# First attention: queries and keys as two fp32r parts, scores on alternating halves of the array's rows

## The reference, cut to what matters

```python
qkv = (x @ Wqkv.T + bqkv).reshape(Bb, Ss, 3, H, HD).transpose(2, 0, 3, 1, 4)
q, k, v = (qkv[0], qkv[1], qkv[2])
attn = jax.nn.softmax(jnp.einsum('bhid,bhjd->bhij', q, k) / jnp.sqrt(jnp.float32(HD)), axis=-1)
...
mod = attn * coh[..., None]
mod = mod / (mod.sum(-1, keepdims=True) + 1e-08)
...
mod = (1.0 - fi) * mod + fi * fa[:, None, :, None]
out = jnp.einsum('bhij,bhjd->bhid', mod, v).transpose(0, 2, 1, 3).reshape(Bb, Ss, Ee)
return out @ Wout.T + bout
```

## Time and profile before

| what | value |
|---|---|
| median of 3 runs | 1663.36 us (1662.22 to 1663.41) |
| the profiled execution's own time | 1665.16 us |
| its span (first to last instruction) | 1663.2 us |
| TensorE busy, share of the span | 1511.5 us, 91% |
| VectorE, ScalarE, POOL busy | 1050.4, 903.7, 496.5 us |
| granted TensorE clock over the span | 0.966 |
| projection | 0 to 105 us |
| first attention | 105.5 to 475.1 us |

### The profile page before, as it was taken

How to read it: one execution, slowest core, us unless ns; L and a number is a source line. 1 busy time by engine, 2 the same in 40 slices (tenths; PEclk the granted TensorE clock), 3 DMA queues, 4 the chain that set the end, 5 groups by cost and what they waited for, 6 DMA issues and landing times. The chain is left out here.

```text
span 1663.2 us, 24878 instructions
## 1 busy us (share of the span) xinstructions
PE 1511.5 (91%) x9076; PEld 988.6 (59%) x9076; DVE 1050.4 (63%) x1915; ACT 903.7 (54%) x1870; POOL 496.5 (30%) x299
## 2 busy tenths in 40 slices
PE   7889999999977999999997689997799689997898
PEld 3432222222234888887874467776577477776676
DVE  3768888888637556464555355555777455555786
ACT  5147777777742434343432487876433477776342
POOL 7100000000015100000002487775312487775113
PEclk9899999999989999999998899999799799999899
DMA  8721212200000330303005200001100100000010
GB/s 244 138 39 20 35 26 39 39 1 1 1 24 2 127 102 5 109 0 114 0 0 174 70 1 1 1 1 49 28 1 0 58 1 2 1 1 26 1 50 25
DMA packets 59312, 64.84 MB, mean 39 GB/s; under 512 B 15091, under 2 KB 48579, under 8 KB 59221
## 3 DMA queue, kind: packets, MB, share of 16 engines
q1 hardware_dynamic: 57860, 60.24, 14.3%
q10 hardware_dynamic: 1360, 3.41, 0.6%
HBM read 52.95 MB, written 10.49 MB: 38 GB/s over the span
## 5 line engine op out<-in xcount | busy, mean ns | idle before, releaser
L577 DVE TENSOR_REDUCE mcol<-bank 128x1 f32<-128x1024 f32 x256 | 302.1, 1217 | 58.5 <-PE bank L568 58.4
L662 ACT ACTIVATE a_pt<-bank 128x512 f32<-128x512 f32 x512 | 266.4, 603 | 89.0 <-PE bank L694 88.9
L694 PE MATMUL bank<-qa,ka 99*128 99x512 bf16 x512 | 193.8, 386 | 7.6 <-ACT a_pt L662 3.8
L568 PE MATMUL bank<-ka,qa 96*128 96x512 bf16 x512 | 193.7, 386 | 5.6 <-DMA ka<-k_parts 2.1
L1639 DVE CUSTOM_DVE_ANT_0 w_sm<-bank,mask 128x256 f32<-128x256 f32 (+1 forms) x256 | 89.0, 404 | 147.5 <-PE bank L1473 147.5
L1831 PE MATMUL bank<-m_hn,m_w 128*128 128x512 f32 x576 | 150.9, 419 | 19.0 <-DVE m_hn L1962 16.4
L1436 PE MATMUL bank<-wqkv,w_hst 128*128 128x512 f32 x576 | 156.4, 420 | 12.5 <-DVE w_sinp L1616 7.6
L694 PEld LDWEIGHTS bank<-qa,ka 99*128 99x128 bf16 x512 | 49.2, 98 | 165.7 <-ACT a_pt L662 121.3
L1831 PEld LDWEIGHTS bank<-m_hn,m_w 128*128 128x128 f32 x576 | 112.4, 196 | 56.0 <-issue 27.2
L705 PE MATMUL bank<-a_pt,vst 128*32 128x512 f32 x1024 | 136.4, 605 | 0.1
L1564 ACT ACTIVATE w_sm<-w_sm,w_st 128x256 f32<-128x256 f32 (+1 forms) x256 | 124.0, 489 | 19.2 <-DVE w_st L1639 19.0
(11 more groups left out here) (231 smaller groups left out, 2766.6 us busy)
## 6 DMA issues: line engine op xcount, KB each, us to landing
f_wex<-in_W SPq DMA_DIRECT2D x8, 2048.0 KB, 12.0
qa<-q_parts SPq DMA_DIRECT2D x48, 128.0 KB, 4.5
ka<-k_parts SPq DMA_DIRECT2D x48, 128.0 KB, 4.7
q_parts<-p_parts SPq DMA_DIRECT2D x16, 192.0 KB, 3.3
k_parts<-p_parts SPq DMA_DIRECT2D x8, 384.0 KB, 3.4
wqkv_raw<-in_wqkv SPq DMA_DIRECT2D x2, 1536.0 KB, 8.8
w<-in_w SPq DMA_DIRECT2D x2, 1536.0 KB, 6.4
phi<-in_phi SPq DMA_DIRECT2D x5, 512.0 KB, 3.6
```

What stands on the lines that cost most here:

```text
L568: last = nc.tensor.matmul(max_bank(G, r)[:, jh * HALF:(jh + 1) * HALF], G["qa"][k][0:KS, hg % 2, h, it * P:(it + 1) * P], G["ka"][k][0:KS, ...
L577: nc.vector.reduce_max(G["mcol"][hg % 2][:, p:p + 1], max_bank(G, r)[:, :], X).then_inc(G["max_free"], 1)
L662: nc.scalar.activation(pt[n % 2][:, q, :], sbank(HG * step + q), ACT.Exp, scale=HD0 ** -0.5).then_inc(p_ready, 1)
L694: mm(sbank(i), ka[k][:, q, n * P:(n + 1) * P], qa[k][:, ih, q, :], start=True, stop=True).then_inc(st_ps, 1)
```

## The change

Queries and keys are written in two fp32r parts, high and rest, in place of three of bf16, and three products of parts in place of six: 3 x 16 = 48 partitions, with two rows of maxima 50. These 50 fit in half of the array's rows. So `qa` holds all queries twice, on partitions 0 to 49 and 64 to 113, and `ka` holds the first 512 keys of a group on the lower half and the last 512 on the upper. The matmuls of a maxima pair go to one half each. The scores of the attention come from the lower and the upper half in turn, the upper lagging two behind; the order of the key tiles in the weighted sum changes with it, and `a_pt` has three buffers. What each engine does is re-ordered accordingly.

ScalarE's second part and POOL's third go; the split of the maxima has two operations for four, and four row DMAs for three. Loads of a group are again twelve DMAs, of fp32; those of the first group go in units 4 to 9. The ones of the keys' side are written over 32 partitions on each half; those of the fourth group (now a buffer that is allocated after the projection) at the start of the attention, and TensorE and SP wait for them there. `p_c1T` lies over the ring of parts, so ScalarE waits for the stores before it writes there.

```diff
-KS = 6 * HD0
-KA = KS + 3
-Q_PART = (0, 0, 1, 1, 0, 2)
-K_PART = (0, 1, 0, 1, 2, 0)
+KS = 3 * HD0
+KA = KS + 2
+ROWS = P // 2
+Q_PART = (0, 0, 1)
+K_PART = (0, 1, 0)
...
-        parts = sb("p_parts", [P, 4, 3, HALF], BF16)
+        parts = sb("p_parts", [P, 4, 2, HALF], F32R)
...
+                sp.wait_ge(G["ones_in"], 2 * GB)
                 for u, (b, hf, m) in enumerate(UNITS):
-                    sp.wait_ge(qk_p3, u + 1)
+                    sp.wait_ge(qk_low, u + 1)
...
-                    if u >= 4:
+                    if 4 <= u < 4 + 2 * len(Q_PART):
                         load_head_parts(sp, G, u % 2, 0, 0, ((u - 4) // 2,))
...
-                for u in range(len(UNITS)):
-                    pool.wait_ge(qk_p2, u + 1)
-                    nc.gpsimd.tensor_tensor(parts[:, u % 4, 2, :], rest[:, u % 4, :], parts[:, u % 4, 1, :],
-                                            ALU.subtract).then_inc(qk_p3, 1)
+                for s in range(GB - 1):
+                    write_ones(nc, pool, G, s)
...
+                for s in range(4):
+                    act.wait_ge(qk_stored[s], STORED[s] * len(UNITS) // 4)
...
+def write_ones(nc, pool, G, k):
+    for d in range(2):
+        nc.gpsimd.memset(G["ka"][k][ROWS * d + 32:ROWS * d + 64, :, :].bitcast(F32), 1.0).then_inc(G["ones_in"], 1)
...
-        last = nc.tensor.matmul(max_bank(G, r)[:, jh * HALF:(jh + 1) * HALF], G["qa"][k][0:KS, hg % 2, h, it * P:(it + 1) * P],
-                                G["ka"][k][0:KS, h, jh * HALF:(jh + 1) * HALF], start=True, stop=True)
+        rows = slice(ROWS * jh, ROWS * jh + KS)
+        last = nc.tensor.matmul(max_bank(G, r)[:, jh * HALF:(jh + 1) * HALF], G["qa"][k][rows, hg % 2, h, it * P:(it + 1) * P],
+                                G["ka"][k][rows, h, :], start=True, stop=True)
...
-        pt = [sb(f"a_pt{s}", [P, HG, HALF]) for s in range(2)]
+        pt = [sb(f"a_pt{s}", [P, HG, HALF]) for s in range(3)]
...
+        EACH = PAIRS * HALVES
+        LAG = 2
...
+        def units(e):
+
+            return [(d, x) for d, x in ((0, e), (1, e - LAG)) if 0 <= x < EACH]
...
+                write_ones(nc, pool, G, GB - 1)
+                pool.wait_ge(G["ones_in"], 2 * GB + 2)
...
+                for e in range(EACH + LAG):
+                    for d, x in units(e):
+                        i, tile = turn_of(d, x), tile_of(d, x)
+                        if tile >= 3 and x % HG == 0:
+                            act.wait_ge(pv_done, tile - 2)
+                        act.wait_ge(st_ps, i + 1)
+                        nc.scalar.activation(pt[tile % 3][:, x % HG, :], sbank(i), ACT.Exp,
+                                             scale=HD0 ** -0.5).then_inc(p_ready, 1)
...
                     if i >= 3:
                         pe.wait_ge(p_ready, i - 2)
-                    mm(sbank(i), ka[k][:, q, n * P:(n + 1) * P], qa[k][:, ih, q, :],
+                    rows = slice(ROWS * d, ROWS * d + KA)
+                    mm(sbank(i), ka[k][rows, q, n * P:(n + 1) * P], qa[k][rows, ih, q, :],
                        start=True, stop=True).then_inc(st_ps, 1)
...
-                pe.wait_ge(G["ones_in"], GB + 2)
...
+                pe.wait_ge(G["ones_in"], 2 * GB + 2)
+                for e in range(EACH + LAG + HG + 1):
+                    hg, x = e // PAIRS, e % PAIRS
+                    ahead, p = (hg + 1, x + EARLY) if x + EARLY < PAIRS else (hg + 2, x + EARLY - PAIRS)
+                    for d, y in units(e):
+                        scores(d, y)
+                    if x == EARLY + 2 and hg + 1 < HALVES:
+                        maxima_to_rows(nc, pe, G, hg + 1)
+                    if ahead < HALVES:
+                        score_pair(nc, pe, G, ahead, p)
+                    if e % 2 == 1 and e >= HG + 1 and (e - HG - 1) // 2 < TT * HALVES:
+                        weighted((e - HG - 1) // 2)
```

More of the change, by code:

```diff
@@ L117, in stage_project @@
         sgn = sb("p_sgn", [16, 16])
[L119 to L121 removed]
+        with nc.sbuf_tensor("p_c1T", [P, KD, N], F32) as c1T:
+            pass
+        parts = sb("p_parts", [P, 4, 2, HALF], F32R)
         cbias = sb("p_cbias", [P, KD, B])
@@ L273, in _ @@
                         nc.scalar.activation(qsd[:, :, :], qn[:, :, :], ACT.Sqrt).then_inc(q_sd, 1)
-                second(len(UNITS) - 1)
                 act.wait_ge(ln_var, 1)
@@ L631, in stage_attention0, with turn_of, tile_of, filled @@
         obank = PB[1][:, HALF:T]
+        EACH = PAIRS * HALVES
+        LAG = 2
+        def turn_of(d, e):
+            return e + max(0, e - LAG) if d == 0 else min(e + LAG + 1, EACH) + e
+        def tile_of(d, e):
+            return e // HG * 2 + d
+        def filled(tile):
+            return turn_of(tile % 2, tile // 2 * HG + HG - 1) + 1
+        def units(e):
+            return [(d, x) for d, x in ((0, e), (1, e - LAG)) if 0 <= x < EACH]
         with nc.Block() as block:
@@ L702, in weighted @@
                             pe.wait_ge(o_out, hg)
-                    pe.wait_ge(p_ready, HG * (step + 1))
+                    pe.wait_ge(p_ready, filled(tile))
                     for q in range(HG):
-                        last = mm(obank[32 * q:32 * q + 32, :], vst[hg // 2 % 2][:, jt, q, :],
-                                  pt[jt % 2][:, q, :], start=(jt == 0), stop=(jt == TT - 1))
+                        last = mm(obank[32 * q:32 * q + 32, :], vst[hg // 2 % 2][:, jt % 2 * (TT // 2) + jt // 2, q, :],
+                                  pt[tile % 3][:, q, :], start=(jt == 0), stop=(jt == TT - 1))
                     last.then_inc(pv_done, 1)
-                pe.wait_ge(G["ones_in"], GB + 2)
-                for hg in range(HALVES):
-                    pe.wait_ge(G["shifted"][hg // 2 % GB], 48 * (2 * (hg // (2 * GB)) + hg % 2 + 1))
-                    for n in range(TT):
-                        ahead = hg + 1 if n < TT // 2 else hg + 2
-                        p0 = (2 * n + EARLY) % PAIRS
-                        for q in range(HG):
-                            scores(hg, n, q)
-                            if n == TT // 2 + 1 and q == 0 and hg + 1 < HALVES:
-                                maxima_to_rows(nc, pe, G, hg + 1)
-                            if ahead < HALVES:
-                                score_pair(nc, pe, G, ahead, p0 + q // 2, (q % 2,))
-                        if hg + n > 0:
-                            weighted(TT * hg + n - 1)
-                weighted(TT * HALVES - 1)
+                pe.wait_ge(G["ones_in"], 2 * GB + 2)
[10 more added lines that the diff above has]
+                        weighted((e - HG - 1) // 2)
 def load_phi(sp, G, A, c):
```

124 lines of the change are left out of this document (54 added, 70 removed).

## The result

The changed kernel takes 1687.8 us (median of four runs: 1677.5, 1686.8, 1688.8 and 1716.5), the kernel before 1663.0 beside it. The ratio is 1.0128, 95% interval 1.0105 to 1.0151: the changed kernel is slower, by 1.3%. The forecast was 1679, the range 1652 to 1700. The other three runs lie 11.3 us apart, where the kernel before has 1.2. The times go with the clock: the fastest run has a mean granted clock of 0.962, the next two 0.952 and 0.953, the one at 1716.5 has 0.930. So the fastest run lies 1.5 us under the forecast, and what the other two take more goes with their lower clock; the sections on the tail and the start show where the profiled one lost it.

The account below looks back on a forecast made before the run. TensorE was taken as the bound before, the chain through three score banks after. Attention +9.2, its start +4.0 and projection +3.3 sum to +16.5 us on the median 1663.4, 1679.9; 1 off for pipeline fill gives 1679, range 1652 to 1700.

Parts of the forecast that it names:

- the third rival: Attention: fp32r matmuls on the two row halves run one after the other, +43 us, 1706; chance 0.13.
- The chain: Attention step: waits through three score banks set the cycle, 2.90 us against 2.85; +5.8 us with maxima, +5.2 without.
- The bare load: Attention: an fp32r weight load not hidden behind a running matmul costs +0.10 us, twice in each cycle's chain.
- The first rival: Attention: the fp32r weight loads are hidden in the wait, -16.6 us there, 1654 in all; chance 0.16.
- Ends of a half: Attention, once a half: transposition wait hidden, first weighted group later; -6.3 and +4.5 us, copies of OT 23.4 us apart.
- the two terms of -6.3 and +4.5: Half ends: -15 x 0.42 us as transposition falls into the bank wait; +15 x 0.3 as the weighted group awaits a copy.
- Start: Start of the attention: TensorE and SP wait for two more memsets on POOL, +4.0 us.
- Projection: Projection: more bytes +4, group 0's keys landing before use -2.1, maxima pairs' mode changes and loads +1.4; sum +3.3 us.
- +10 if DMA alone sets the pace: Projection: upper case for the wait before unit 15, 8.6 MB through DMA for 5.8, before deductions that leave +5 us.
- The clock: Attention: rival that TensorE's idling drops its clock to 1.2 GHz, up to +205 us; chance 0.06.
- the fill of the pipeline: Start of the attention: first maxima pairs overlap at the low clock; left out of the sum, then 1 us taken off.
- Packing's full factor: Attention: rival that VectorE becomes the bound, 19.1 us a half, -59 us, 1611 in all; chance 0.05.

Follow-up runs that it names:

- Run 1: Changed kernel with the maxima pair ahead of the scores on TensorE's queue in every second turn: 1671.8 us, ratio 1.0033 to the kernel before.
- run 2: Changed kernel with two bf16 parts in place of two fp32r, so less precise products: 1635.9 us, ratio 0.9834 to the kernel before.
- run 10: Changed kernel with maxima ahead in every second turn, tail filler matmuls, no TensorE wait for the fourth group's ones, first group's loads spread: 1665.8 us.
- run 3: Changed kernel with unread filler pairs of 48-row matmuls in the attention's tail, where no maxima are left: 1683.8 us, ratio 1.0109 to the kernel before.
- run 4: Changed kernel with all score and maxima matmuls on the lower half of the rows, so none overlap and results differ: 2008.9 us.
- run 6: Changed kernel with tail filler, plus 14 unread matmuls on all rows at the start of the attention: 1680.9 us.
- runs 8 and 9: Changed kernel with maxima ahead, tail filler, no fourth-group wait, full-row matmuls in the first 16 turns; with 14 more ahead 1669.2 us, without 1672.4.

## Why the prediction was right, and where not

The sign was right and the measured time lies in the range. The size was 9 us short of the median of four, and 8 short of the median of the other three. In the profiled execution, 21.9 us were measured and 15.5 forecast: the tail and the start took 11 to 12 us more than the sum had, the thirteen halves 1 less, and the stages behind gave 3.5 back. That the range held is in part luck: its upper part stood for the third rival, no overlap, and was used up by the clock.

- **The chain, right.** Forecast 2.90 us a cycle with maxima and 2.67 without. Measured 2.83 to 2.91 (2.88 in the mean), and without maxima, before the clock fell, 2.66 and 2.62 (pairs at 457.26, 459.92 and 462.54). Run 1 shortened one leg and the copies moved from 23.37 to 22.2; run 2 shortened two legs.
- **The bare load, right.** 0.10 us forecast, 0.10 and 0.12 measured in two legs (run 2). The first rival had the right lever: without that price thirteen halves are 22 us shorter. The rest of what run 2 gained came from the projection and the clock, which this rival didn't name.
- **Ends of a half, right in sum.** 23.4 forecast, 23.37 measured. The longer step at the end of a half takes 0.35 more than a regular one, where the kernel before has 0.43 and the two terms of -6.3 and +4.5 together say 0.3; they were not measured apart.
- **Start, right.** +4.0 forecast, 3.65 for the memsets; run 10 took 3.5 away.
- **Projection, right in sum.** +3.3 forecast, +3.2 measured. The high part of unit 15 starts at 48.5 us for 43.6, +4.9 where +4 was forecast, and TensorE's wait for the first keys, 2.1 us, is gone as forecast. Line L253 of the changed kernel waits for stores:

```profile
  DMA k_parts<-p_parts: 12.8, 6
...
  DMA q_parts<-p_parts: 6.2, 4
```

  19.0 us in all, where the earlier trace rows had 5.7 for the queries' stores and the kernel before 2.1 more for the keys'. The first store goes out at 13.2 us for 17.3, and still unit 15 is 4.9 late: nine us were lost between for 2.8 MB more, 3.2 us for each MB. Run 2 halved the prediction's 8.6 MB and had the high part of unit 15 at 38.8 us, 9.7 earlier, 2.3 for each MB. Both are estimates, and TensorE's granted clock from 10 to 50 us was not the same (0.92 before, 0.93 changed, 1.00 in run 2). They lie somewhat below the "+10 if DMA alone sets the pace" of the prediction, which is 3.6 for each MB. The other 3.2 of run 2's 12.9 us came behind unit 15; their cause is open.
- **The clock, wrong.** This is the step that failed. The prediction put it at nothing in its sum. It gave it a chance of 0.06 and argued from the earlier trace rows, 1.00 with TensorE busy 86%. It held busy time for the thing to compare. In the tail the changed kernel was busy 87% and fell to 0.50; a step there took 4.07 us for 2.64. Its price in the tail of the profiled executions is 10.5 us (run 3). At the start, where the sum took 1 us off for the fill of the pipeline, the stretch from the first score to the first copy of OT grew by 2.5, with the clock at 0.50 until about 122 us; how much of this the clock made, and how much the lag of the upper half, was not measured apart. The Trainium skill, TensorE: Matmul & The Clock Gate, Part 1: The HAM clock gate, ties the rate to how busy the engine has been; here the trace differs, since 340 us at 100% busy left it at 0.50 (run 4).
- **Packing's full factor, wrong as a rival.** The array's columns were saved, and the time didn't move with them: the same columns in another order gave 16 us. Only when load and order were both mended did VectorE come near to being the bound, the place that this rival named.

Open: why bf16 on the two halves kept the clock in the tail (busy 81% from 408 to 446 us) and fp32r didn't in the profiled runs, and what decides from run to run how long the low clock lasts at the start.

## What to carry to other kernels

When an array's work shrinks, look in the trace for a stretch where that work is already absent: the step's time there is the chain that will become the bound, and here its legs gave the new step as 2.90 us for 2.88. Then order the instructions so that nothing stands in that chain which could run in its wait, and prefer operands whose weight load is short wherever a matmul follows a wait. Matmuls on part of the rows may also cost the clock, so compare the granted clock in each stretch, and the spread of the runs, and not the busy share alone.

## What the hardware showed that I had not expected

- One half of the rows at a time: granted clock 0.50 for the whole attention with TensorE busy 100%, in fp32r (340 us) and in bf16 (355 us). The clock rose with 99 rows in the kernel before, with all 128 in runs 6 and 8, and with both halves at once in the changed kernel; which property of the work decides is not shown.
- With fp32r on both halves the level at the start differs from run to run: at 0.50 until about 122 us in the changed kernel's profile, 145 in run 10's and 170 in run 3's. The spread goes with it: 19 us in run 3, 25 with pairs as filler, 1.4 with work on all rows ahead (run 6), 4 to 5 in runs 8 and 9, 3 with bf16. These are four to six runs each.
- Two matmuls on the two halves are issued 3 ns apart, and the second adds nothing to the path that I could see.
- A MB more of DMA in the projection, at 316 GB/s from 10 to 50 us, cost 2.3 to 3.2 us, by the estimates above; from the kernel before to the changed one the median landing of a store of the queries grew from 3.3 us (192 KB) to 6.7 us (256 KB).
